# Gated delta-rule layer on one core: key products of two chunks side by side in one bank, and the triangular inverse built up from the identity

## The chip, the cores and the metric

The kernel runs on one core of one Trainium2 chip. The metric is the time on the device in microseconds (us) for one execution, as the median over several runs. Before the change it is 2536.91 us (three runs, 2536.58 to 2537.79).

## What is computed

The input x has 4 sequences of 512 tokens with 256 features. After a layer norm it goes through a gated delta rule with 16 query/key heads, each shared by 2 value heads of 128 features, and through a small gated feed-forward part whose weights come from a table of 16 numbers; the result is x plus the product of both. The part that matters here, for every pair of sequence and value head, works on chunks of 64 tokens:

```python
q, k = rmsnorm(q) * inv, rmsnorm(k) * inv              # and q, k, v from a conv and silu
decay = where(tril, exp(g[..., :, None] - g[..., None, :]), 0.0)
M = where(stril, einsum('bhncd,bhnmd->bhncm', k_beta, k) * decay, 0.0)
T = solve_triangular(eye + M, eye, lower=True)          # 64 x 64 for each chunk
v_c, k_cumdecay = T @ v_beta, T @ (k_beta * exp(g))
# then a scan over the 8 chunks: attn = (q_i @ k_i^T) * dec_i, v_new = v_i - kcd_i @ state, ...
```

## The kernel before, in words

The work is cut into 32 rounds. A round takes one query/key head and two of the four sequences (BB = 2), and so 8 chunks (NC = 8) of each of two sequences for two value heads (RATIO = 2). The two value heads lie in the two halves of the 128 partitions, 64 rows (C = 64) each. In a round each engine goes through the same three parts, in an order written out by hand, and the engines meet by semaphores: `invert`, `recur`, and `begin` of the following round.

- `begin` makes what the inverse needs. TensorE multiplies keys by keys and queries: tile `kq` holds for each chunk the keys twice and the queries once (3 x 64 columns). L481 takes the 128 columns with the doubled keys as weights and the 128 columns of keys and queries as moving data. So the product stands in both partition halves, one copy for each value head, 4 chunks in a PSUM bank, 4 banks in all (uses "kkq"). VectorE multiplies the key part of each bank by -DB (decay and beta) into U (L1009) and by -DB0 (the same, only for pairs of neighbouring tokens) into X (L1010). ScalarE copies the query part into A (L792). GpSimd has made DB0 from DB earlier, in `first_level` (L1180). After its 4 banks VectorE scales the last output block of the round before (`scale_o(last, 3)`, L1093, tile `on`), adds the identity to X (L1018), does `gated(last, 3)` (L1104) and turns X into W within the blocks (L1033).
- TensorE goes on in `begin` with the turned keys (L487, uses "kt", copied out by ScalarE at L783 into Kd), then `turn_back(last, 3)` (L641), which waits for `scale_o(last, 3)`, then the turned values (L494, uses "vt", copied out by ScalarE at L800 into V with a factor for each row). Then follow three of the four output products of the round before (L651).
- `invert` doubles the inverted blocks in 5 levels: two groups of 64 by 64 products in each (L462 and L464, then L467 and L469), with a ScalarE copy of the first result (L814), a masked copy of the second into X by VectorE (L1045), a turn (L1033), and `swap`, a ScalarE copy of X with the halves exchanged (L836). Beside the levels TensorE makes the projections of the next round (L413), ScalarE and VectorE their convolution (`tap0` L732, `taps` L948).
- `recur` is the scan over the chunks (L591, L599, L617, L564, L569 on TensorE; L1064, L1083, L961 and others on VectorE; squares for the output norm on ScalarE, L855; Sd at L1188 and small powers at L1204, L1214 on GpSimd).

A PSUM bank is handed over by counters: `wait_open` waits until the last reader is through with it, `wait_full` until TensorE has filled it. Which use lies in which bank is set in `bank_uses`. The weights `w_o`, `w_qkv` and the small rows come by DMA from SyncE's queue; the constants (identity, masks) are one transfer at the start, which ScalarE, TensorE and GpSimd wait for. TensorE also increments a semaphore `tiled` ahead of each group of 64 by 64 products; nothing waits for it.

Of the kernel before, what the change touches and what calls it, by code (L numbers as in the profile page):

```python
# [9 lines left out]
I32 = mybir.dt.int32  # L10
# [68 lines left out]
def constants():  # L79
# [3 lines left out]
    cols.append(((j // 2 == i // 2) & (j % 2 == 0) & (i % 2 == 1)) * 1.0)  # L83
    for lv in range(1, LEVELS):
# [9 lines left out]
NCONST = 2 * P + C + C + (LEVELS - 1) * HALF + C + 4  # L94
# [35 lines left out]
def build(nc, x, consts, resets_in, wqkvz, wba, convw, dtb, alog, normw, wout, lut, idx, out):  # L130
# [3 lines left out]
    with ExitStack() as ctx:  # L134
# [22 lines left out]
        DB0 = sb("DB0", [P, BB, NC, C])  # L157
# [32 lines left out]
        def flat(t, n=None):  # L190
# [7 lines left out]
        first_mask = cst[:, 2 * P + C:2 * P + 2 * C]  # L198
        masks = [cst[:, 2 * P + 2 * C + HALF * n:2 * P + 2 * C + HALF * (n + 1)] for n in range(LEVELS - 1)]
# [13 lines left out]
                 "normed_o dec_pool dec_small ss_c dec_act qg_c sd_c kg_c a_c u_c xs eye_c st_c x_c o_sq ff_gu ff_gate ff_h ff_y ff_sy fin x_again stored tiled").split()  # L213
# [42 lines left out]
        gw = [t for buf in (DB, DB0, Dm) for t in (flat(buf, S)[:, 0, :], flat(buf, S)[:, 1, :])]  # L256
# [9 lines left out]
        def _(sp):  # L266
# [56 lines left out]
            def body(R):  # L323
# [10 lines left out]
                if R.par == 1 and not R.nxt:  # L334
                    wait_read(sp, R, "kkq", 3)
# [33 lines left out]
        def _(pe):  # L369
# [75 lines left out]
            def products(banks, lv, first):  # L445

                pe.sem_inc(s["tiled"], 1)
# [96 lines left out]
            def keys_through(R):  # L544

                for b in range(BB):
# [3 lines left out]
                    pe.sem_inc(s["tiled"], 1)  # L550
# [23 lines left out]
            def recur(R):  # L574
# [3 lines left out]
                for b in range(BB):  # L578
                    bank, filled = wait_open(pe, R, "vn", b)
                    pe.sem_inc(s["tiled"], 1)  # L580
# [4 lines left out]
                for c in range(NC):  # L585
# [22 lines left out]
                    if c < NC - 1:  # L608
                        _, s_filled = wait_open(pe, R, "sp", c)
                        for b in range(BB):  # L610
                            wait_read(pe, R, "vn", c * BB + b)
                            pe.sem_inc(s["tiled"], 1)
# [7 lines left out]
                    else:  # L620
                        for b in range(BB):
                            wait_read(pe, R, "vn", c * BB + b)
                        pe.sem_inc(s["tiled"], 1)
# [81 lines left out]
        def _(act):  # L705
            act.wait_ge(s["ld_const"], 16 * n_const)
            for t in range(NT):
                act.wait_ge(s["ln_stat"], 2 * (t + 1))
                act.activation(std[:, t:t + 1], mv[:, t, 1:2], ACT.Sqrt, bias=eps[:, 0:1]).then_inc(s["ln_std"], 1)
# [43 lines left out]
            def decays(R):  # L753
                par = 0 if R.head else 1 - R.par
                act.wait_ge(s["dec_pool"], R.at(1, 9, 9))
# [6 lines left out]
                for b in range(BB):  # L762
                    act.wait_ge(s["dec_pool"], R.at(3 + 2 * b, 9, 9))
# [22 lines left out]
            def begin(R):  # L786
                for i in range(4):
                    act.wait_ge(s["u_c"], R.at(i + 1, 0, 4))
                    n, _ = R.use("kkq", i)
                    b, c4 = i // 2, slice((i % 2) * 4, (i % 2) * 4 + 4)  # L790
                    src = ps[n][:, :].rearrange("p (c t) -> p c t", t=P)
                    act.activation(A[:, b, c4, :], src[:, :, C:P], ACT.Copy).then_inc(read[n], 1)  # L792
# [3 lines left out]
                for i in range(4):  # L796
                    bank, done = wait_full(act, R, "vt", i)
                    for u in range(4):
                        c = (i % 2) * 4 + u
                        m = act.activation(V[:, i // 2, c, :], bank[:, u * P:(u + 1) * P], ACT.Copy,  # L800
                                           scale=rinv[:, i // 2, c:c + 1])
                    m.then_inc(done, 1)
                swap(R, 0)

            def invert(R):
                for lv in range(1, LEVELS):
# [31 lines left out]
            def body(R):  # L838
# [36 lines left out]
        def _(dve):  # L875
# [124 lines left out]
            def begin(R, last=None):  # L1000

                dve.wait_ge(s["dec_pool"], R.at(0, 9, 9))
# [31 lines left out]

            def invert(R):
                if R.before() is not None:
                    outputs(R.before(), (3,))
                for lv in range(1, LEVELS):
                    done = [wait_full(dve, R, "p2", (lv, b))[1] for b in range(BB)]
                    n = 1 << lv  # L1040

                    odd = X[:, :, :, :].rearrange("p b c (q d n) -> p b (c q) d n", d=2, n=n)[:, :, :, 1, :]

                    dve.memset(carry[:, 1:2], 0.0)
# [289 lines left out]
```

## Time and profile before

| | |
|---|---|
| median of 3 runs | 2536.91 us |
| the profiled execution, its own time | 2537.4 us |
| its span, first to last instruction | 2535.6 us |
| mean granted TensorE clock | 0.99 of full |
| busy: TensorE, weight loads, VectorE, ScalarE, GpSimd | 95%, 73%, 66%, 56%, 71% |
| one round in the middle of the run | 71.9 us |

The profile comes from one execution. "PE" is TensorE's products, "PEld" its weight loads, which overlap them, "DVE" is VectorE, "ACT" ScalarE, "POOL" GpSimd. A row of instructions gives how many there were, how long one took, and in square brackets how long the engine had been idle before it and what ended that. The chain of waits is followed back from the last instruction: at each step to what released it. In float32 most products are two instructions in the records, so 16 products are "x32".

### The profile page before, as it was taken

The page shows a single profiled execution, that of the slowest core. Times are in us where ns is not written, and L with a number is a line of the kernel's source. Part 1 is how long each engine was busy: PE and PEld are TensorE (multiplying, and loading weights), DVE is VectorE, ACT ScalarE, POOL GpSimd, SP SyncE. Part 2 cuts the span into 40 slices and gives each one's busy share as a digit, 9 for nine tenths or more (in the row PEclk, how much of TensorE's full clock was granted, in tenths as well). Part 3 has the DMA queues.
Part 4 walks back from the last instruction along what each step waited for, and adds up shares of the span by engine and source line. Part 5 has one row for each costly group of instructions (what it writes and reads, how often), then busy time and mean ns, then how long its engine had stood idle before and what let it go on. Part 6 is the DMA issues. An engine that isn't in the chain of part 4 may idle for free.

```text
span 2535.6 us, 102175 instructions
## 1 busy us (share of the span) xinstructions
PE 2403.8 (95%) x44496; PEld 1858.4 (73%) x44496; DVE 1663.7 (66%) x2955; ACT 1424.9 (56%) x3237; POOL 1809.7 (71%) x1838
## 2 busy tenths in 40 slices
PE   4899999999999999999999999999999999999899
PEld 3687777777877777777777777777777777776544
DVE  6666676667666766677666766676667666775322
ACT  2665565665656656656556566555566566564211
POOL 2787777778877777788777777787777777887200
PEclk8899999999999999999999999999999999999999
DMA  3111110111111101111111101111111011111100
GB/s 114 34 36 37 38 34 18 34 43 30 37 37 38 38 13 39 34 43 30 36 39 34 31 21 43 34 34 36 38 39 34 18 34 43 30 37 26 49 17 17
DMA packets 71051, 89.94 MB, mean 35 GB/s; under 512 B 16720, under 2 KB 39376, under 8 KB 70480
## 3 DMA queue, kind: packets, MB, share of 16 engines
q1 hardware_dynamic: 70608, 83.40, 12.4%
q8 instruction: 355, 5.82, 0.9%
q14 instruction: 88, 0.72, 0.1%
HBM read 78.30 MB, written 5.08 MB: 33 GB/s over the span
## 4 chain that ended last, share of the span: by engine, by line
PE 66%; DVE 23%; issue 5%; ACT 4%; DMA 1%; POOL 0%; DVEq 0%; SPq 0%; ACTq 0%; POOLq 0%
PE ps_two L433 9%; PE ps_two L651 9%; PE ps_two L413 9%; DVE cacc L948 7%; PE ps_p L591 5%; DVE XW L1033 3%; PE ps_state L617 3%; PE ps_two L641 3%; PE ps_p L467 3%; PE ps_two L425 3%; ACT cacc L732 3%; DVE hT L1104 3%; PE ps_p L481 2%; DVE Vn L1064 2%; PE ps_p L599 2%
## 5 line engine op out<-in xcount | busy, mean ns | idle before, releaser
L1188 POOL TENSOR_TENSOR Sd<-St,el 128x512 f32<-128x512 f32 x192 | 201.3, 1048 | 455.9 <-ACT eg L758 358.4
L1226 POOL TENSOR_SCALAR hT<-idx_s,lutb 128x134 f32<-128x134 int32 x480 | 355.5, 744 | 27.1
L1064 DVE TENSOR_SCALAR Vn<-ps_p,bR 128x128 f32<-128x128 f32 x512 | 165.3, 348 | 266.9 <-PE ps_p L564 180.0
L836 ACT ACTIVATE Xs<-XW 64x512 f32<-64x512 f32 x320 | 201.1, 628 | 233.2 <-DVE XW L1045 227.6
L948 DVE SCALAR_TENSOR_TENSOR cacc<-ps_two,cw,cacc 128x1022 f32<-128x1022 f32 (+2 forms) x192 | 243.1, 1266 | 73.0 <-ACT cacc L732 69.9
L948 DVE SCALAR_TENSOR_TENSOR cacc<-ps_state,cw,cacc 128x1022 f32<-128x1022 f32 (+2 forms) x192 | 244.3, 1273 | 31.1 <-ACT cacc L732 13.5
L413 PE MATMUL ps_state<-xnT,w_qkv 128*128 128x256 f32 x1024 | 257.1, 395 | 5.9 <-DVEq L953 5.9
L433 PE MATMUL ps_two<-xnT,w_z 128*128 128x512 f32 x512 | 244.4, 610 | 8.9 <-DVEq L953 8.2
L413 PE MATMUL ps_two<-xnT,w_qkv 128*128 128x256 f32 x1024 | 247.0, 389 | 0.0
L651 PE MATMUL ps_two<-w_o,hT 128*128 128x256 f32 x1024 | 236.3, 384 | 0.0
L1033 DVE STREAM_TRANSPOSE XW<-XW 128x1024 f32<-128x1024 f32 x160 | 199.3, 1245 | 36.5 <-DVE XW L1045 31.5
L462 PEld LDWEIGHTS ps_p<-XW,U 64*64 64x64 f32 (+1 forms) x5120 | 156.5, 130 | 76.6 <-issue 76.2
L413 PEld LDWEIGHTS ps_state<-xnT,w_qkv 128*128 128x128 f32 x1024 | 185.9, 191 | 34.6 <-DVEq L953 6.3
L651 PEld LDWEIGHTS ps_two<-w_o,hT 128*128 128x128 f32 x1024 | 190.6, 191 | 25.0
L855 ACT ACTIVATE P<-ps_p 128x128 f32<-128x128 f32 x256 | 67.2, 277 | 249.8 <-PE ps_p L569 249.8
L413 PEld LDWEIGHTS ps_two<-xnT,w_qkv 128*128 128x128 f32 x1024 | 187.4, 190 | 27.5
L467 PEld LDWEIGHTS ps_p<-XW,P 64*64 64x64 f32 (+1 forms) x5120 | 151.8, 129 | 71.0 <-issue 71.0
L591 PE MATMUL ps_p<-St,Kg 128*64 128x128 f32 x1792 | 161.3, 292 | 34.1 <-DVE St L1083 30.6
L462 PE MATMUL ps_p<-XW,U 64*64 64x32 f32 (+1 forms) x5120 | 173.6, 215 | 18.0 <-DVE XW L1033 13.3
L1199 POOL TENSOR_TENSOR qg<-qg,kq 128x512 f32<-128x512 f32 x128 | 190.7, 1522 | 0.0
L1083 DVE TENSOR_TENSOR St<-Sd,ps_state 128x256 f32<-128x256 f32 x384 | 144.4, 417 | 49.6 <-PE ps_state L617 19.1
L1113 DVE TENSOR_TENSOR acc<-acc,ps_two 128x512 f32<-128x512 f32 x128 | 86.8, 678 | 135.5 <-PE ps_two L651 135.5
(166 smaller groups left out, 6237.5 us busy)
## 6 DMA issues: line engine op xcount, KB each, us to landing
qg<-g_scratch SPq DMA_DIRECT2D x64, 512.0 KB, 7.3
g_st<-g_scratch SPq DMA_DIRECT2D x64, 256.0 KB, 5.6
w_qkv<-in_wqkvz SPq DMA_DIRECT2D x16, 512.0 KB, 3.8
w_z<-in_wqkvz SPq DMA_DIRECT2D x16, 256.0 KB, 3.1
w_o<-in_wout SPq DMA_DIRECT2D x16, 256.0 KB, 2.7
idx_s<-in_idx SPq DMA_DIRECT2D x32, 67.0 KB, 1.8
fw_scratch<-looked_up SPq DMA_DIRECT2D x32, 67.0 KB, 1.7
Kg<-in_x SPq DMA_DIRECT2D x2, 1024.0 KB, 6.0
```

What stands on the lines that cost most here:

```text
L413: m = pe.matmul(bank[:, t0:t0 + S // 2], w_qkv[:, k, kind * P:(kind + 1) * P], rows, start=(k == 0), stop=(k == KD - 1))
L433: m = pe.matmul(bank[:, :], w_z[:, k, a * P:(a + 1) * P], xnT[:, k, cols(R.par, b)], start=(k == 0), stop=(k == KD - 1))
L462: left = pe.matmul(to(0, m_same), U[k_same, 0, c, ins], halves(W[k_same, 0, c, :], lv, 0), start=True, stop=True)
L467: left = pe.matmul(to(0, k_same), P1[m_same, 0, c, k0:k0 + kn], halves(X[m_same, 0, c, :], lv, 1), start=True, stop=True)
L591: m = pe.matmul(olds[b][0][r, 0:P], Kg[:, b, c, r], St[:, cur, b, a, :], start=False, stop=True, skip_group_check=True)
L651: m = pe.matmul(bank[:, b * D:(b + 1) * D], hT[:, t, b, 1 - a, :], w_o[:, a, :], start=(a == 0), stop=(a == RATIO - 1))
L836: act.activation(Xs[(1 - a) * C:(2 - a) * C], X[a * C:(a + 1) * C, 1], ACT.Copy).then_inc(s["x_c"], 1)
L948: dve.scalar_tensor_tensor(dst, both[n][:, :, 0:S - t], cw[:, kind, 3 - t:4 - t], dst, ALU.mult, ALU.add).then_inc(s["taps"], 1)
L1033: dve.transpose(flat(W), flat(X)).then_inc(xs, 1)
L1064: dve.tensor_scalar(Vn[:, cur, b], bank[:, 0:P], bR[:, R.par, b, c:c + 1], None, ALU.mult).then_inc(done, 1)
L1188: pool.tensor_tensor(Sd[:, :, :, :], St[:, c % 2, :, :, :], el[:, R.par, :, :, c].unsqueeze(3).broadcast_to([P, BB, RATIO, P]), ALU.mult). ...
L1226: m = pool.tensor_scalar(slots[k], idx_s[:, :], float(k), lutb[:, k:k + 1], ALU.is_equal, ALU.mult)
```

## The change

Key products: each chunk's product now has only 64 weight columns, and two chunks stand side by side in the partition halves of one bank, so that 2 banks hold what 4 held. VectorE and ScalarE read each half and write it to both halves of U and A. The first level of the inverse no longer goes through DB0: ScalarE writes the identity into all blocks of X (once at the start, and near the end of each `recur`), and VectorE lays the odd rows of U over it with a masked copy. The mask of that level becomes as long as those of the others, 512 columns for 64. DB0 and its GpSimd work go. ScalarE copies half of the turned values in `begin`, the other half inside level 1. The increments of `tiled` go, here and at five more places in `keys_through` and `recur`. The banks of "kt" and "vt" are dealt out anew.

```diff
-    begin = (spread([("kkq", i) for i in range(4)], (4, 5, 6, 7)) + spread([("kt", i) for i in range(4)], (2, 4, 5, 6))
-             + spread([("vt", i) for i in range(4)], (3, 7, 2, 4)))
+    begin = (spread([("kkq", b) for b in range(BB)], (4, 5)) + spread([("kt", i) for i in range(4)], (2, 6, 7, 4))
+             + spread([("vt", i) for i in range(4)], (3, 5, 7, 6)))
...
-NCONST = 2 * P + C + C + (LEVELS - 1) * HALF + C + 4
+NCONST = 2 * P + C + LEVELS * HALF + C + 4
...
@@ TensorE, products @@
-                pe.sem_inc(s["tiled"], 1)
...
@@ TensorE, begin @@
-                for i in range(4):
-                    bank, filled = wait_open(pe, R, "kkq", i)
+                for b in range(BB):
+                    bank, filled = wait_open(pe, R, "kkq", b)
                     for u in range(4):
-                        c = (i % 2) * 4 + u
-                        m = pe.matmul(bank[:, u * P:(u + 1) * P], kq[:, i // 2, c, 0:P], kq[:, i // 2, c, C:3 * C],
-                                      start=True, stop=True)
+                        for side in range(2):
+                            c = side * 4 + u
+                            m = pe.matmul(bank[side * C:(side + 1) * C, u * P:(u + 1) * P], kq[:, b, c, 0:C],
+                                          kq[:, b, c, C:3 * C], start=True, stop=True)
                     m.then_inc(filled, 1)
...
@@ ScalarE @@
+            def clear_inverse():
+                act.activation(X[:, :].rearrange("p b c i -> p (b c) i"), eye.unsqueeze(1).broadcast_to([P, BB * NC, C]),
+                               ACT.Copy).then_inc(s["eye_c"], 1)
+
+            clear_inverse()
...
             def begin(R):
-                for i in range(4):
-                    act.wait_ge(s["u_c"], R.at(i + 1, 0, 4))
-                    n, _ = R.use("kkq", i)
-                    b, c4 = i // 2, slice((i % 2) * 4, (i % 2) * 4 + 4)
-                    src = ps[n][:, :].rearrange("p (c t) -> p c t", t=P)
-                    act.activation(A[:, b, c4, :], src[:, :, C:P], ACT.Copy).then_inc(read[n], 1)
+                for b in range(BB):
+                    bank, _ = wait_full(act, R, "kkq", b)
+                    for side in range(2):
+                        act.wait_ge(s["u_c"], R.at(2 * b + side + 1, 0, 4))
+                        src = bank[side * C:(side + 1) * C, :].rearrange("p (c t) -> p c t", t=P)[:, :, C:P]
+                        for a in range(RATIO):
+                            m = act.activation(A[a * C:(a + 1) * C, b, side * 4:side * 4 + 4, :], src, ACT.Copy)
+                    m.then_inc(read[R.use("kkq", b)[0]], 1)
                 for i in range(4):
                     copy_turned(R, "kt", i, Kd)
                 act.wait_ge(s["rinv_c"], R.at(0, 1, 1))
-                for i in range(4):
+                values(R, 0)
+                swap(R, 0)
...
@@ ScalarE, invert: after the copy of level 1 @@
+                    if lv == 1:
+                        values(R, 1)
...
@@ ScalarE, recur part of body @@
+                    if c == NC - 1 and R.nxt:
+                        for b in range(BB):
+                            wait_full(act, R, "vn", (NC - 1) * BB + b)
+                        clear_inverse()
...
@@ VectorE, begin @@
-                for i in range(4):
-                    if i == 2 and last is not None:
+                for b in range(BB):
+                    if b == 1 and last is not None:
                         gated(last, 2)
-                    bank, _ = wait_full(dve, R, "kkq", i)
-                    b, c4 = i // 2, slice((i % 2) * 4, (i % 2) * 4 + 4)
-                    src = bank[:, :].rearrange("p (c t) -> p c t", t=P)[:, :, 0:C]
-                    dve.scalar_tensor_tensor(U[:, b, c4], src, -1.0, DB[:, b, c4, :], ALU.mult, ALU.mult)
-                    dve.scalar_tensor_tensor(X[:, b, c4], src, -1.0, DB0[:, b, c4, :], ALU.mult, ALU.mult
-                                             ).then_inc(s["u_c"], 1)
+                    bank, _ = wait_full(dve, R, "kkq", b)
+                    for side in range(2):
+                        c4 = slice(side * 4, side * 4 + 4)
+                        src = bank[side * C:(side + 1) * C, :].rearrange("p (c t) -> p c t", t=P)[:, :, 0:C]
+                        for a in range(RATIO):
+                            r = slice(a * C, (a + 1) * C)
+                            m = dve.scalar_tensor_tensor(U[r, b, c4], src, -1.0, DB[r, b, c4, :], ALU.mult, ALU.mult)
+                        m.then_inc(s["u_c"], 1)
                 if last is not None:
                     scale_o(last, 3)
                 for b in range(BB):
                     dve.wait_ge(s["u_c"], R.at(2 * b + 2, 0, 4))
-                over_all = eye.unsqueeze(1).broadcast_to([P, BB * NC, C])
-                x_all = X[:, :].rearrange("p b c i -> p (b c) i")
-                dve.tensor_tensor(x_all, x_all, over_all, ALU.add).then_inc(xs, 1)
+                dve.wait_ge(s["eye_c"], R.at(1, 0, 1))
+                into_odd(0, odd(U, 0)).then_inc(xs, 1)
...
+            def into_odd(lv, src):
+
+                dve.memset(carry[:, 1:2], 0.0)
+                mask = masks[lv].rearrange("p (b q n) -> p b q n", b=BB, n=1 << lv)
+                return dve.copy_predicated(odd(X, lv), mask.bitcast(I32), src)
...
@@ GpSimd @@
-            def first_level(R, b):
-                pool.wait_ge(s["dec_pool"], R.at(5 + b + 1, 9, 9))
-                pool.tensor_tensor(DB0[:, b, :, :], DB[:, b, :, :], first_mask.unsqueeze(1).broadcast_to([P, NC, C]),
-                                   ALU.mult).then_inc(s["dec_pool"], 1)
```

## Rows read from the trace of the kernel before

**Rows 1.** The page: shares of the chain of waits by engine.

```profile
PE 66%; DVE 23%; issue 5%; ACT 4%; DMA 1%; POOL 0%; DVEq 0%; SPq 0%; ACTq 0%; POOLq 0%
```

**Rows 2.** Chain of waits in one round: start us, us, what ended last there.

```profile
1018.50 1.80 PE ps_p L481 x16
...
1023.96 0.66 PE ps_two L641 x4
...
1026.36 5.18 PE ps_two L651 x24
...
1039.42 1.12 ACT cacc L732
```

**Rows 3.** Timeline of TensorE's weight loads there: start us, us, in brackets the idle time.

```profile
1023.12 0.47 PEld L487 LDWEIGHTS ps_state<-cst,kq 128*128 128x128 f32 x4
1023.95 0.42 PEld L641 LDWEIGHTS ps_two<-cst,on 128*128 128x128 f32 x4 [0.37 <-DVE on L1093]
...
1025.21 0.91 PEld L494 LDWEIGHTS ps_p<-cst,vs 128*128 128x128 f32 x8
```

**Rows 4.** The same chain at changes between product shapes.

```profile
1008.41 0.39 PE ps_p L591 x4
...
1016.76 0.44 PE ps_p L599 x8
...
1017.26 0.65 PE ps_p L569 x8
1017.92 0.59 PE ps_two L641 x4
...
1035.60 3.67 PE ps_two L413 x16
```

**Rows 5.** Timeline of VectorE through `begin`.

```profile
1019.52 0.42 DVE L1009 SCALAR_TENSOR_TENSOR U<-ps_p,DB 128x256 f32<-128x256 f32 x1 [0.86 <-PE ps_p L481]
...
1021.00 0.74 DVE L1104 SCALAR_TENSOR_TENSOR hT<-ps_two,gpar,z 128x512 f32<-128x512 f32 x1
1021.89 0.42 DVE L1009 SCALAR_TENSOR_TENSOR U<-ps_state,DB 128x256 f32<-128x256 f32 x1
...
1022.89 0.41 DVE L1010 SCALAR_TENSOR_TENSOR XW<-ps_state,DB 128x256 f32<-128x256 f32 x1
1023.22 0.68 DVE L1093 TENSOR_TENSOR on<-ps_p,rr 128x512 f32<-128x512 f32 x1
```

**Rows 6.** VectorE at L961, four in a row, each on other partition halves: together, and each.

```profile
1001.80 0.74 DVE L961 TENSOR_SCALAR kn<-ps_two 64x8 f32<-64x8 f32 x4
...
L961 DVE TENSOR_SCALAR kn<-ps_two x4: 146/164/170, 1001.8 to 1002.4; 64x8 f32<-64x8 f32 x4
```

**Rows 7.** Timeline of ScalarE through `begin` and level 1.

```profile
1017.95 0.28 ACT L855 ACTIVATE P<-ps_p 128x128 f32<-128x128 f32 x1 [3.73 <-PE ps_p L569]
...
1023.34 0.38 ACT L792 ACTIVATE A<-ps_state 128x256 f32<-128x256 f32 x1 [0.28 <-DVE XW L1010]
1023.62 1.57 ACT L783 ACTIVATE Kd<-ps_p 128x512 f32<-128x512 f32 x3
1025.05 0.63 ACT L783 ACTIVATE Kd<-ps_state 128x512 f32<-128x512 f32 x1
...
1027.52 2.27 ACT L800 ACTIVATE V<-ps_p,rinv 128x128 f32<-128x128 f32 x8
1029.81 1.28 ACT L836 ACTIVATE Xs<-XW 64x512 f32<-64x512 f32 x2
```

**Rows 8.** VectorE's and GpSimd's work that goes: by line, count, ns or total us.

```profile
L1018 DVE TENSOR_TENSOR XW<-XW,cst x32: 2039/2260/2314, 85.2 to 2319.0; 128x1024 f32<-128x1024 f32 x32
...
L1180 POOL TENSOR_TENSOR DB<-DB,cst 128x512 f32<-128x512 f32 x64 | 81.6, 1275 | 0.0
```

**Rows 9.** The start: the constants' transfer, and pieces of the chain of waits.

```profile
cst<-in_consts SPq DMA_DIRECT2D x1, 1506.0 KB, 11.0
...
87.50 4.11 ACT V L800 x16
```

More of the change, by code:

```diff
@@ L82, in constants @@
     cols = [np.eye(P), np.ones((P, P)), (j == i) * 1.0]
-    cols.append(((j // 2 == i // 2) & (j % 2 == 0) & (i % 2 == 1)) * 1.0)
-    for lv in range(1, LEVELS):
+    for lv in range(LEVELS):
         n = 1 << lv
@@ L197, in build @@
         eye = cst[:, 2 * P:2 * P + C]
-        first_mask = cst[:, 2 * P + C:2 * P + 2 * C]
-        masks = [cst[:, 2 * P + 2 * C + HALF * n:2 * P + 2 * C + HALF * (n + 1)] for n in range(LEVELS - 1)]
+        masks = [cst[:, 2 * P + C + HALF * n:2 * P + C + HALF * (n + 1)] for n in range(LEVELS)]
         causal = cst[:, NCONST - 4 - C:NCONST - 4]
@@ L212, in build @@
                  "ba_act g_c g_dup g_tr g_sc g_out fw_c fw_st ld_fw ld_fd zeroed tap0 taps silu sq n2_c rinv_c inv_o turned scaled "
-                 "normed_o dec_pool dec_small ss_c dec_act qg_c sd_c kg_c a_c u_c xs eye_c st_c x_c o_sq ff_gu ff_gate ff_h ff_y ff_sy fin x_again stored tiled").split()
+                 "normed_o dec_pool dec_small ss_c dec_act qg_c sd_c kg_c a_c u_c xs eye_c st_c x_c o_sq ff_gu ff_gate ff_h ff_y ff_sy fin x_again stored").split()
         s = {n: sem(n) for n in names}
@@ L255, in build @@
         scs = flat(z)[:, 0:1024].rearrange("p (k h b c) -> p k h b c", k=2, h=HQK, b=B)
-        gw = [t for buf in (DB, DB0, Dm) for t in (flat(buf, S)[:, 0, :], flat(buf, S)[:, 1, :])]
+        gw = [t for buf in (DB, U, Dm) for t in (flat(buf, S)[:, 0, :], flat(buf, S)[:, 1, :])]
         resets = flat(P1, S)[:, 1, :]
@@ L334, in body @@
                 if R.par == 1 and not R.nxt:
-                    wait_read(sp, R, "kkq", 3)
+                    wait_read(sp, R, "kkq", 1)
                     wait_read(sp, R, "kt", 3)
@@ L549, in keys_through @@
                     banks = [wait_open(pe, R, "kcd", 2 * b + a) for a in range(RATIO)]
-                    pe.sem_inc(s["tiled"], 1)
                     for c in range(NC):
@@ L579, in recur @@
                     bank, filled = wait_open(pe, R, "vn", b)
-                    pe.sem_inc(s["tiled"], 1)
                     for a in range(RATIO):
@@ L611, in recur @@
                             wait_read(pe, R, "vn", c * BB + b)
-                            pe.sem_inc(s["tiled"], 1)
                             for a in range(RATIO):
@@ L622, in recur @@
                             wait_read(pe, R, "vn", c * BB + b)
-                        pe.sem_inc(s["tiled"], 1)
                     for b in range(BB):
@@ L795, in begin, with values @@
                 act.wait_ge(s["rinv_c"], R.at(0, 1, 1))
-                for i in range(4):
+                values(R, 0)
+                swap(R, 0)
+            def values(R, b):
+                for i in range(2 * b, 2 * b + 2):
                     bank, done = wait_full(act, R, "vt", i)
@@ L799, in begin @@
                         c = (i % 2) * 4 + u
-                        m = act.activation(V[:, i // 2, c, :], bank[:, u * P:(u + 1) * P], ACT.Copy,
-                                           scale=rinv[:, i // 2, c:c + 1])
+                        m = act.activation(V[:, b, c, :], bank[:, u * P:(u + 1) * P], ACT.Copy,
+                                           scale=rinv[:, b, c:c + 1])
                     m.then_inc(done, 1)
-                swap(R, 0)
             def invert(R):
@@ L1033, in turn, with odd @@
                 dve.transpose(flat(W), flat(X)).then_inc(xs, 1)
+            def odd(t, lv):
+                return t[:, :, :, :].rearrange("p b c (q d n) -> p b (c q) d n", d=2, n=1 << lv)[:, :, :, 1, :]
+            def into_odd(lv, src):
+                dve.memset(carry[:, 1:2], 0.0)
+                mask = masks[lv].rearrange("p (b q n) -> p b q n", b=BB, n=1 << lv)
+                return dve.copy_predicated(odd(X, lv), mask.bitcast(I32), src)
             def invert(R):
@@ L1170, in with_beta @@
                 if not R.head and b == 0:
-                    wait_full(pool, R, "kkq", 3)
+                    wait_full(pool, R, "kkq", 1)
                     pool.wait_ge(s["u_c"], R.at(4, 0, 4))
@@ L1253, in attention @@
                 for b in range(BB):
-                    wait_read(pool, R, "kkq", 2 * b + 1)
+                    wait_read(pool, R, "kkq", b)
                     pool.tensor_tensor(A[:, b], A[:, b], Dm[:, b], ALU.mult).then_inc(s["a_c"], 1)
@@ L1260, in _ @@
                 with_beta(HEAD, b)
-            for b in range(BB):
-                first_level(HEAD, b)
             lengths(HEAD)
@@ L1277, in body @@
                         with_beta(R, c - 3)
-                    elif R.nxt and c > 4:
-                        first_level(R, c - 5)
                 if R.nxt:
```

15 lines of the change are left out of this document (5 added, 10 removed).

## The prediction

> **What bounds the kernel now.** I read the chain of waits first. TensorE holds 66% of it, VectorE 23% [rows 1]. A faster TensorE stage therefore pays only where no other engine ends the wait behind it. So I cut out one round, around `begin`, where the change lies, and asked of each engine when it starts what.
>
> The chain of waits goes there through the first key bank, then leaves TensorE: VectorE's eight products, `gated(last, 2)` and `on` follow and end at 1023.90 [rows 5], and only then `turn_back` (L641) runs. From 1023.96 TensorE holds the chain without a gap through the turned values, the outputs and level 1, until ScalarE's `tap0` at 1039.42 [rows 2]. The reader should see the handover: TensorE was through with loading the turned keys at 1023.12 + 0.47 = 1023.59 and its loads sat idle 0.37 us for `on` [rows 3]. TensorE, 95% busy over the run, has slack exactly where its work is cut, and whatever delays `on` moves the round. There are 31 such handovers between 32 rounds, and the weight loads' idle time ahead of L641 recurs in other rounds.
>
> **Key products on TensorE.** Now 16 products in 32 records, 16 of them in 1.80 us, so all in 3.6 us [rows 2]. After, 16 products with 64 weight columns in 8 pairs. The nearest row is L599: 4 products of this shape (64 columns, 128 moving) in 0.44 us on the chain [rows 4], 0.22 a pair. So 8 pairs cost 1.76 and save 1.8 us of TensorE's time. They bring a change of shape. In rows 4 the first pair after one takes 0.39 for 0.22 (L591 behind L641), so 0.17 us. The first bank, with 4 pairs, is full after 0.17 + 0.88 = 1.05 us, where the old one with 4 products took 0.90: VectorE starts 0.15 later, at 1019.67. The 1.8 us come out behind this, ahead of a wait for `on`, and give nothing by themselves. The Trainium skill ("TensorEngine Tiling (Array Packing)", Key Properties) says that a change of tiling mode drains TensorE; the 0.17 us agree with that. Its section on the PSUM bottleneck says that such packing doesn't speed up evacuation, and that is the case here by the handover of rows 2.
>
> **VectorE's eight products.** Their number stays 8, two for each old bank before, four for each new bank after, 256 elements each as before. Half the partitions don't shorten one; I keep 0.42 us. What changes is how they follow one another. Now they overlap: a piece that starts at 1022.89 and takes 0.41 is followed at 1023.22, 0.33 later, by `on` [rows 5]. The new ones read and write changing partition halves. The only row with this very pattern (half by half from PSUM, written to both halves) is L961: four take 0.74 together, 0.164 each, so (0.74 - 0.164) / 3 = 0.192 from start to start, 0.03 more than the length [rows 6]. They don't overlap. ScalarE's L836 shows the same: two take 1.28, so 0.64 each or a little more, against (1025.05 - 1023.62) / 3 = 0.48 from start to start for L783's full-height copies of the same 512 elements [rows 7]. I take 0.42 + 0.03 = 0.45 for each of the eight; the other bound is 0.335, as now. Between them I choose by L961, whose pattern is the same.
> The Trainium skill ("VectorE: DVE Perf Modes", Two Vector instructions with no wait between them) says that an instruction whose start quadrant differs from the last one's, in what it reads or writes, starts only when all earlier ones have finished. By it every new product is held, which gives the sum below; L961's spacing agrees. If it failed here, the time would be that of rival 1.
>
> VectorE's clock: 1019.67 + 4 x 0.45 = 1021.47; `gated` 0.89 to the next start (1021.00 to 1021.89, rows 5) 1022.36; 4 x 0.45 gives 1024.16, where `on` started at 1023.22. So `on`, and L641 with it, comes 0.94 us later.
>
> **ScalarE and the banks.** The second turned-value group of TensorE's last four (L494 x8) needs "vt" 2 in bank 7, where "kt" 2 stands until ScalarE has copied it; before, it needed "kt" 0, copied long ago. ScalarE: last U piece starts at 1023.71, ends 1024.13; the copy into A starts 0.04 later as now (1022.89 + 0.41 to 1023.34), then again, each 0.38 + 0.02 without overlap; "kt" 0 starts at 1024.98, "kt" 2 two steps of 0.48 later at 1025.94, and ends 0.61 after that (1.57 for three less two steps), at 1026.55 [rows 7]. TensorE would be there at 1025.21 + 0.94 = 1026.15 [rows 3]. It waits until 1026.60 and then needs 0.66 + 0.44 = 1.10 us for the two groups (restart as L641, then as L599's 0.44) and ends at 1027.70, where it ended at 1026.36 before. **The handover costs 1.34 us a round.** Bounds of the ScalarE part alone: nothing if its copies keep pace, 0.4 as worked here. Behind it everything up to `tap0` is TensorE's own time, so nothing takes the delay back.
>
> **The rest.** (a) L1018, 2.26 us [rows 8], becomes a masked copy of 512 elements. It lies behind `on`; the turned X is wanted at 1031.5, VectorE has it by 1028.5 before and after, so nothing. If that cover of 3 us were gone it would gain 1 to 1.5 us. (b) GpSimd loses two L1180 a round, 2.55 us [rows 8]. It only comes to its powers and `scale_q` earlier; `on` isn't waiting for it. Nothing. (c) ScalarE's identity, 1024 elements, 1.1 us as `tap0`, as large [rows 2], waits for the last Kg product (done at 1016.76, where L599 begins, rows 4) and runs until 1017.9, in the 3.73 us of idleness ahead of L855 at 1017.95 [rows 7]. Nothing, at most 0.1 on the squares, whose result has 2 us of slack. (d) Eight of the 16 copies into V, half of 16 x 0.283 us (L800's 2.27 for 8, rows 7), move behind level 1's copy: ScalarE waits there for X until 1037. Hidden. (e) Removing `tiled`: into 64 by 64 shapes, with the increment, the first group costs 0.65 - 0.43 = 0.22 (L569); without it, into full shape, 0.59 - 0.43 = 0.16 (L641) and 3.67 - 3.41 = 0.26 (L413, 16 of 0.213) [rows 4]. No difference, so nothing; bounds 0 and 0.04 us for each of 29 in a round, of which about 20 lie on the path. (f) Start: 224 KB more constants on 1506 KB in 11.0 us [rows 9], +1.6 at most, the first identity +1.0, against 4.11 / 2 = 2.05 less ahead of the first level [rows 9] and some 1 us of products at the low clock. Together 0, within 3.
>
> **Sum.** 2537.4 (the profiled execution; span 2535.6) + 31 x 1.34 = 41.5 gives 2578.9. The runs' median lies 0.5 below that execution: 2578.4, so 2578 us.
>
> **Rivals.**
> 1. *VectorE's products keep overlapping.* Then `on` is late by 0.15 - 0.14 (the small wait for the second bank goes) = 0.01 only; "kt" 2 is copied by 1025.48 and TensorE loses 0.27 us: 31 x 0.27 = 8.4, 2545 us. For: the pieces share no data. Against: L961's and L836's spacing. Chance 0.12, with what lies between it and the forecast.
> 2. *Faster: the removed increments were not free.* They stand in TensorE's queue, and a standing cost of 0.04 us each, 20 on the path, 32 rounds, is 26 us; with rival 1's small loss the time is 2519. Its place is ahead of L462, L467, L617; it decides the sign once it exceeds what the handover costs. Against: rows 4 show no dearer entry with it. The other way to gain, that TensorE's saved 1.8 us show (31 x 1.8 = 56 us, 2481), needs `on` to be early, against 0.37 us of waiting for it [rows 3]. Chance of both 0.10.
> 3. *The pairs don't run side by side*, the edit does not do what it says. Then the first bank is full 0.88 us later again and the handover costs 2.2 us: 2606. Against: L599. Chance 0.04.
> 4. *About no change*, gains and losses cancelling: 0.04.
>
> The forecast has 0.70. A measurement of this kernel can tell about 0.2%, 5 us, from no change. The range goes down to rival 1 (2545) and up to 1.8 us a round, 0.5 us a piece in place of 0.45 and the late start in full, 2593. Faster 0.10, same 0.05 (rival 4 and a part of rival 1), slower 0.85.
>
> **What would show it.** L1009's new pieces: 8 a round, 0.42 long, 0.45 apart, where overlap would show 0.34. TensorE's loads idle about 3 us ahead of L641, ended by `on`, and again about 0.4 ahead of L494, ended by ScalarE's Kd. L481 in 8 pairs at 0.22. Rounds of 73.2 us for 71.9. Wrong I would be if the pieces were shorter than 0.42, or if the rounds were shorter while `on` is late: then a cost that I put at nothing, `tiled` first, was one.

## The result and the profile after

The changed kernel takes 2604.35 us (median of 4, 2602.49 to 2605.87) against 2536.76 for the kernel before; the ratio is 1.0265, 95% interval [1.0247, 1.0283]. It is slower by 67.6 us, where 41 us were forecast. The direction and the place were right, the size was not: the time lies above the range, which ended at 2593.

The page after, its span, granted clock in 40 slices and chain of waits, against [rows 1]:

```profile
span 2604.1 us, 101789 instructions
...
PEclk8999999999999999999999999999999999999999
...
PE 62%; DVE 25%; issue 5%; ACT 4%; DVEq 0%; DMA 0%; ACTq 0%; POOL 0%; POOLq 0%; SPq 0%
```

The slices are too coarse for what counts. The mean granted clock is 0.977, where it was 0.990.

Here is one handover between rounds, in the timeline of the weight loads (start us, us, idle time in brackets). It answers to [rows 3], with 102.00 us between corresponding moments of the two traces (the loads of the turn before the key products start at 1017.85 and at 1119.85):

```profile
1119.85 0.42 PEld L634 LDWEIGHTS ps_two<-cst,on 128*128 128x128 f32 x4 [0.17 <-DVE on L1109]
1120.44 1.73 PEld L478 LDWEIGHTS ps_p<-kq 128*64 128x64 f32 x32 [0.17 <-issue]
...
1124.27 0.42 PEld L484 LDWEIGHTS ps_p<-cst,kq 128*128 128x128 f32 x4 [0.64 <-ACT A L792]
1126.86 0.42 PEld L634 LDWEIGHTS ps_two<-cst,on 128*128 128x128 f32 x4 [2.18 <-DVE on L1109]
...
1128.54 0.86 PEld L491 LDWEIGHTS ps_state<-cst,vs 128*128 128x128 f32 x8 [0.39 <-ACT Kd L782]
1129.37 0.73 PEld L644 LDWEIGHTS ps_two<-w_o,hT 128*128 128x128 f32 x4
```

The wait for `on` grew from 0.37 to 2.18 us, and there are two new ones, 0.64 for the bank that ScalarE's A copies free and 0.39 for "kt" 2. VectorE's timeline over the same stretch, as in [rows 5]:

```profile
1121.67 1.75 DVE L1023 SCALAR_TENSOR_TENSOR U<-ps_p,DB 64x256 f32<-64x256 f32 x4 [1.04 <-PE ps_p L478]
1123.45 0.75 DVE L1120 SCALAR_TENSOR_TENSOR hT<-ps_two,gpar,z 128x512 f32<-128x512 f32 x1
1124.34 1.74 DVE L1023 SCALAR_TENSOR_TENSOR U<-ps_p,DB 64x256 f32<-64x256 f32 x4
1126.12 0.69 DVE L1109 TENSOR_TENSOR on<-ps_p,rr 128x512 f32<-128x512 f32 x1
```

and ScalarE's, as in [rows 7]:

```profile
1118.83 1.06 ACT L702 ACTIVATE XW<-cst 128x1024 f32<-128x1024 f32 x1 [2.65 <-PE ps_p L586]
1119.96 0.28 ACT L866 ACTIVATE P<-ps_p 128x128 f32<-128x128 f32 x1
...
1125.28 1.61 ACT L792 ACTIVATE A<-ps_p 64x256 f32<-64x256 f32 x4 [1.07 <-DVE U L1023]
```

Four pieces take 1.75 us, so (1.75 - 0.42) / 3 = 0.44 from start to start. The identity (L702) fits exactly before the squares. In this handover the forecast is met to a tenth: pieces from 1121.67 - 102.00 = 1019.67 (forecast 1019.67), L634's loads from 1024.86 (1024.89), the second pair of turned values from 1026.54 (1026.60). The interval from this round's first piece back to the one before is long, 75.03 us, the next one is 73.20, the length that I had forecast for all.

The next handover looks like this:

```profile
1197.47 0.42 PEld L484 LDWEIGHTS ps_p<-cst,kq 128*128 128x128 f32 x4 [0.64 <-ACT A L792]
1200.07 0.54 PEld L634 LDWEIGHTS ps_two<-cst,on 128*128 128x128 f32 x4 [2.18 <-DVE on L1109]
1200.60 1.72 PEld L491 LDWEIGHTS ps_p<-cst,vs 128*128 128x128 f32 x8
1202.30 1.60 PEld L491 LDWEIGHTS ps_state<-cst,vs 128*128 128x128 f32 x8
```

The waits are the same, but the turned values' loads take 1.72 us, where before the change they took 0.91 [rows 3]. The stretches of the two handovers, with each engine's busy time and, ahead of the DMA share, the granted clock:

```profile
1125.00:1129.00 4.00, 1.98 (x16) 1.75 (x17) 3.64 (x7) 3.60 (x9) 3.25 (x3) 1.00 0.80 192
...
1199.00:1203.00 4.00, 2.93 (x15) 2.93 (x16) 3.54 (x6) 3.89 (x11) 3.25 (x3) 0.66 0.83 163
1203.00:1207.00 4.00, 4.00 (x21) 3.64 (x20) 1.37 (x2) 3.92 (x9) 4.00 (x3) 0.91 0.53 150
```

In the second TensorE is at its lower level, 1.2 GHz instead of 2.4, for (1 - 0.66) x 4 / 0.5 + (1 - 0.91) x 4 / 0.5 = 3.4 us. What it did before was to idle 2.2 us. After this wait TensorE works without a pause until level 1, some 9 us, so half of the 3.4 us, 1.7, is lost. The 0.39 us for "kt" 2 fall away in return, as in the rows above, and the round gets longer by 1.3. Of the 30 intervals between first pieces from 152.94 to 2382.99 us, 7 are 73.2 to 73.3 us, all without low clock, and 23 are 74.4 to 75.2, each with one stretch of 3.4 us. The wait for `on` is 2.2 us in every handover but one (2.5), so the same wait does not always bring the clock down. The low clock is the term that the forecast did not have.

### The profile page after: what moved, and what is told of

It is laid out like the page before. It is cut to its first block, busy times and chain, and to the rows that moved or that the text cites. A ratio compares the mean times of both kernels' runs of the same rounds, so it can differ in the third digit from the quotient of the medians.

```text
span 2604.1 us, 101789 instructions
## 1 busy us (share of the span) xinstructions
PE 2392.6 (92%) x44496; PEld 1826.4 (70%) x44496; DVE 1658.2 (64%) x2987; ACT 1514.8 (58%) x3398; POOL 1707.2 (66%) x1774
## 4 chain that ended last, share of the span: by engine, by line
PE 62%; DVE 25%; issue 5%; ACT 4%; DVEq 0%; DMA 0%; ACTq 0%; POOL 0%; POOLq 0%; SPq 0%
PE ps_two L430 9%; PE ps_two L644 9%; PE ps_two L410 8%; DVE cacc L959 8%; PE ps_p L586 5%; DVE U L1023 4%; DVE XW L1045 3%; PE ps_state L611 3%; PE ps_two L634 3%; PE ps_p L463 3%; ACT cacc L731 3%; DVE hT L1120 3%; PE ps_two L422 3%; DVE Vn L1080 2%; PE ps_p L594 2%
## 5 line engine op out<-in xcount | busy, mean ns | idle before, releaser
L644 PE MATMUL ps_two<-w_o,hT 128*128 128x256 f32 x1024 | 243.3, 392 | 0.0
L644 PEld LDWEIGHTS ps_two<-w_o,hT 128*128 128x128 f32 x1024 | 197.8, 199 | 26.6
L410 PEld LDWEIGHTS ps_state<-xnT,w_qkv 128*128 128x128 f32 x1024 | 186.3, 192 | 37.3 <-DVEq L964 12.0
L458 PEld LDWEIGHTS ps_p<-XW,U 64*64 64x64 f32 (+1 forms) x5120 | 150.5, 129 | 66.4 <-DVE XW L1045 45.5
L458 PE MATMUL ps_p<-XW,U 64*64 64x32 f32 (+1 forms) x5120 | 168.2, 215 | 9.6 <-DVE XW L1045 5.7
L463 PE MATMUL ps_p<-XW,P 64*64 64x32 f32 (+1 forms) x5120 | 168.7, 215 | 1.9 <-ACTq L822 1.9
L465 PE MATMUL ps_p<-Xs,P 64*64 64x32 f32 (+1 forms) x5120 | 169.1, 216 | 0.0
```

The source lines that it names most:

```text
L410: m = pe.matmul(bank[:, t0:t0 + S // 2], w_qkv[:, k, kind * P:(kind + 1) * P], rows, start=(k == 0), stop=(k == KD - 1))
L458: left = pe.matmul(to(0, m_same), U[k_same, 0, c, ins], halves(W[k_same, 0, c, :], lv, 0), start=True, stop=True)
L463: left = pe.matmul(to(0, k_same), P1[m_same, 0, c, k0:k0 + kn], halves(X[m_same, 0, c, :], lv, 1), start=True, stop=True)
L644: m = pe.matmul(bank[:, b * D:(b + 1) * D], hT[:, t, b, 1 - a, :], w_o[:, a, :], start=(a == 0), stop=(a == RATIO - 1))
```

## The experiments

Each kernel is the changed one with one edit, if not said otherwise; each time is a median of at least 4 runs. The kernel before took 2536.6 to 2537.7 us beside them.

**The increments of `tiled` put back** (29 in a round).

```diff
             def products(banks, lv, first):
+                pe.sem_inc(s["tiled"], 1)
...
                     bank, filled = wait_open(pe, R, "vn", b)
+                    pe.sem_inc(s["tiled"], 1)
```

> The changed kernel with the 29 increments of `tiled` a round put back. My theory (they cost nothing; the loss is the late `on` plus stretches of low clock behind TensorE's idle time): 2604 us, within 4. Rival (the increments held TensorE's order or its shape changes in a good way, so their removal is part of the loss): 2585 us or less. Rival (they cost something and their removal gave a hidden gain): 2620 to 2630 us.

2607.88 us, ratio 1.0277 [1.0260, 1.0294], which overlaps the changed kernel's. The increments are worth nothing that can be measured, in either direction.

**TensorE's idle time filled with products.**

```diff
-                    for u in range(4):
+                    for u in range(4 * (6 if i == 3 and last is not None else 1)):
+                        u = u % 4
                         m = pe.transpose(bank[:, u * P:(u + 1) * P], kq[:, i // 2, (i % 2) * 4 + u, 0:P], ident)
```

> The changed kernel, but TensorE turns the last group of keys six times instead of once, into the same bank, so that about 2.1 of the 2.3 us of idle time ahead of `turn_back(last, 3)` are filled with products; nothing that another engine does is changed, and the result is the same. My theory (the low clock, some 23 stretches of 3.4 us at half, follows on the idle time): the stretches go, `on` is as late as before, rounds of 73.2 us, so 2604 - 23 x 1.3 = 2574 us. Rival (the narrow paired products themselves, or something else in the stage, lower the clock): the stretches stay, 2604 us or more, as the added products lie in idle time. If the filling delays L634 itself: up to 0.3 us a round more than that.

2574.69 us, ratio 1.0143 [1.0128, 1.0159], mean granted clock 0.993. The same moment in the timeline of the weight loads:

```profile
1109.94 1.67 PEld L485 LDWEIGHTS ps_p<-cst,kq 128*128 128x128 f32 x15
1111.60 0.44 PEld L635 LDWEIGHTS ps_two<-cst,on 128*128 128x128 f32 x4
```

and the stretch behind it, with the granted clock (1.00) ahead of the DMA share:

```profile
1112.00:1116.00 4.00, 3.87 (x28) 3.43 (x27) 3.11 (x3) 3.98 (x13) 3.28 (x3) 1.00 0.99 241
```

Work that nobody needs makes the kernel 29.7 us faster. VectorE's and ScalarE's work is unchanged, so `on` comes as late as before; only the idle time is gone, and with it the low clock between rounds. This divides the loss: 2574.7 - 2536.8 = 37.9 us at full clock, for which 41 were forecast, and 29.7 us for the clock.

**The banks of the last two turned-value groups exchanged** ("vt" in banks 3, 5, 6, 7 for 3, 5, 7, 6).

> The changed kernel with the banks of the last two turned-value groups exchanged, so that the third waits for `kt` 1 and not `kt` 2 to be copied. My theory (this wait costs 0.38 us a round by the trace of the changed kernel): TensorE's second wait goes, 31 x 0.38 = 12 us less, 2592 us, and down to 2575 if fewer stretches of low clock follow. Rival (the wait is covered, the round is set by `on` alone): 2604 us.

2598.26 us, 6 less. The wait is gone (L491's second group starts at 1124.84, right behind the first), but it gave half of the 12 us:

```profile
1123.58 0.42 PEld L634 LDWEIGHTS ps_two<-cst,on 128*128 128x128 f32 x4 [2.17 <-DVE on L1109]
1123.96 0.91 PEld L491 LDWEIGHTS ps_p<-cst,vs 128*128 128x128 f32 x8
1124.84 0.91 PEld L491 LDWEIGHTS ps_state<-cst,vs 128*128 128x128 f32 x8
```

The trace of the changed kernel shows why. Where the low clock starts early, its first group takes 1.72 us, and by then "kt" 2 is copied, as the rows at 1200.60 and 1202.30 show. The wait for it stands in only 14 of the 31 handovers (in 7 of the 23 with a low stretch), and 14 x 0.39 = 5.5 us. Without this wait to cover, a low stretch costs its full 1.7 us: the rounds here take 72.8 us at full clock (a few 73.2) and 74.5 or more with the stretch. The mean clock stayed at 0.978.

**`scale_o(last, 3)` ahead on VectorE, nothing else.**

```diff
                     if b == 1 and last is not None:
+                        scale_o(last, 3)
                         gated(last, 2)
...
-                if last is not None:
-                    scale_o(last, 3)
```

> The changed kernel with `scale_o(last, 3)` moved ahead on VectorE and nothing else. Theory A (two things are late, `on` and ScalarE's copies that free the banks of the turned values): `turn_back` runs 2 us earlier, but the turned values wait for ScalarE, whose last copies into A now start 0.3 us later; TensorE idles as long, in another place: 2595 to 2615 us. Rival B (`on` is the only cause): 2535 to 2560 us.

2629.57 us, above both ranges. `on` is no longer waited for, and the idle time has moved behind it, larger than I had worked out:

```profile
1056.88 0.42 PEld L634 LDWEIGHTS ps_two<-cst,on 128*128 128x128 f32 x4 [0.53 <-issue]
1057.27 0.47 PEld L491 LDWEIGHTS ps_p<-cst,vs 128*128 128x128 f32 x4
1059.45 0.42 PEld L491 LDWEIGHTS ps_p<-cst,vs 128*128 128x128 f32 x4 [1.72 <-ACT A L792]
1061.05 1.55 PEld L491 LDWEIGHTS ps_state<-cst,vs 128*128 128x128 f32 x8 [1.18 <-ACT Kd L782]
```

`on` in front of the second group of pieces pushes that group back by its whole 0.84 us, and ScalarE's A copies and "kt" copies with it; I had put 0.3. Here 31 x 0.8 = 25 us, the measured difference; the low clock costs as much as before (18 stretches of 1.7 us in 30 rounds for 23 of 1.3). So `on` alone is not the cause. The chain is VectorE's pieces, ScalarE's copies, banks.

**`gated(last, 2)` moved into VectorE's 1.04 us of idle time ahead of the first key bank.**

```diff
                 dve.wait_ge(s["dec_pool"], R.at(0, 7, 7))
+                if last is not None:
+                    gated(last, 2)
                 for b in range(BB):
-                    if b == 1 and last is not None:
-                        gated(last, 2)
```

> The changed kernel with one move: VectorE does `gated(last, 2)` while it waits for the first key bank (1.04 us idle there) instead of between its two groups of pieces. `on`, and ScalarE's copies behind the second group, come 0.9 us earlier. My theory (VectorE's chain up to `on` sets the round, and the length of TensorE's idle time the low clock): 31 x 0.9 = 28 us less by the chain, 2576 us, and if the shorter idle time of 1.4 us no longer brings the clock down, 30 more, 2546 us. Rival (ScalarE or the banks set the round): less than 10 us saved.

2546.86 us, ratio 1.0041 [1.0028, 1.0054]: 57.5 us less from one moved call, as worked out with both terms. The timeline of the weight loads in one handover:

```profile
1094.48 0.42 PEld L484 LDWEIGHTS ps_p<-cst,kq 128*128 128x128 f32 x4 [0.72 <-ACT A L792]
1096.18 0.42 PEld L634 LDWEIGHTS ps_two<-cst,on 128*128 128x128 f32 x4 [1.28 <-DVE on L1109]
```

and the stretch around it, with the granted clock (1.00) ahead of the DMA share:

```profile
1094.00:1098.00 4.00, 2.32 (x17) 1.85 (x18) 3.63 (x7) 3.70 (x10) 4.00 (x4) 1.00 0.90 164
```

With 1.28 us idle for 2.18 the clock stays whole (mean 0.994), and no low stretch lies between the first and the last handover. The rounds take 72.4 us for 73.2, so 31 x 0.8 = 25 us come from the chain and the clock's 30 us on top.

**The change's inverse without its key products**: full-height banks and VectorE's four full-height pieces, the rest as changed, except that all V copies stay in `begin` (with these banks the split would make TensorE and ScalarE wait for each other).

```diff
-                    for side in range(2):
-                        c4 = slice(side * 4, side * 4 + 4)
-                        src = bank[side * C:(side + 1) * C, :].rearrange("p (c t) -> p c t", t=P)[:, :, 0:C]
-                        for a in range(RATIO):
-                            r = slice(a * C, (a + 1) * C)
-                            m = dve.scalar_tensor_tensor(U[r, b, c4], src, -1.0, DB[r, b, c4, :], ALU.mult, ALU.mult)
-                        m.then_inc(s["u_c"], 1)
+                    b, c4 = i // 2, slice((i % 2) * 4, (i % 2) * 4 + 4)
+                    src = bank[:, :].rearrange("p (c t) -> p c t", t=P)[:, :, 0:C]
+                    dve.scalar_tensor_tensor(U[:, b, c4], src, -1.0, DB[:, b, c4, :], ALU.mult, ALU.mult
+                                             ).then_inc(s["u_c"], 1)
```

> The kernel before with its four full-height key banks, and of the change only the inverse from the identity (no DB0, ScalarE's identity, masked copy; all V copies stay in `begin`; no increments). VectorE has 4 full-height pieces in place of 8, so `on` comes 4 x 0.33 = 1.3 us earlier than before and TensorE no longer waits for it. My theory (the half-height pieces are what made the change slower): no slower than before; the 0.37 us of waiting goes, some 0.2 to 0.4 us a round, 2525 to 2532 us, clock as before. Rival (the identity, its wait or the first masked copy cost something): above 2540 us.

2525.34 us, ratio 0.9949 [0.9935, 0.9964]: faster than both kernels. The wait for `on` is gone:

```profile
1019.03 0.47 PEld L483 LDWEIGHTS ps_state<-cst,kq 128*128 128x128 f32 x4
1019.47 0.47 PEld L633 LDWEIGHTS ps_two<-cst,on 128*128 128x128 f32 x4
```

The inverse from the identity is worth 11 us by itself; VectorE has half as many pieces ahead of `on`, the wait for it goes, and rounds take 71.6 us for 71.9. The key products, with their banks and the split of the V copies, gave this away and 68 us more.

**Half-height pieces in two orders**, on that kernel. Each full-height piece is cut into its partition halves (source and target in the same half), once alternating, once with the half kept for two or more in a row. The diff shows the orders of (bank, half) in the two groups.

```diff
+(((0, 0), (0, 1), (1, 0), (1, 1)), ((0, 0), (0, 1), (1, 0), (1, 1)))
...
+(((0, 0), (1, 0), (1, 1), (0, 1)), ((0, 1), (1, 1), (1, 0), (0, 0)))
```

> The full-height key banks and identity inverse (2525 us), but each of VectorE's four full-height pieces is cut into its two partition halves, in the order low, high, low, high. Nothing else halves; ScalarE and TensorE have full height. My theory (a piece that changes partition half does not overlap with the one before): 8 pieces 0.44 us apart, four take 1.75, as in the changed kernel; `on` about 2 us later than with four pieces and TensorE waits for it: 2555 to 2575 us. Rival (what kept the pieces apart in the changed kernel is something else, the mixed source and target halves or the bank shared by two chunks): pieces 0.33 apart, at most 2540 us.

> The same eight half-height pieces of the same lengths, in an order that keeps the half for two or more in a row (low, low, high, high, then high, high, low, low). My theory (only the change of half is held): inside a half 0.33 us apart, at the change 0.44; four take 1.55 for 1.75, so `on` comes 0.3 to 0.4 us earlier than in the alternating order, 8 to 15 us less than it. Rival (half-height pieces are never overlapped): the same time as the alternating order, within 3 us.

2601.76 and 2584.20 us. First the pieces, a group of four in each order (alternating, then grouped):

```profile
1046.72 1.75 DVE L1019 SCALAR_TENSOR_TENSOR U<-ps_p,DB 64x256 f32<-64x256 f32 x4 [1.75 <-PE ps_p L477]
```

```profile
1039.53 1.53 DVE L1019 SCALAR_TENSOR_TENSOR U<-ps_p,DB 64x256 f32<-64x256 f32 x4 [1.75 <-PE ps_p L477]
```

1.75 and 1.53 us were worked out as 1.75 and 1.55. Inside a half the pieces overlap as full-height ones do (0.34 or 0.35 us from start to start), at a change they do not (0.42 to 0.45), and this holds with source and target in one half and one chunk in a bank. So the size of a piece is not the reason, the change of half is. The Trainium skill ("VectorE: DVE Perf Modes", Two Vector instructions with no wait between them) says that an instruction with another start quadrant than the last one's waits until the earlier ones have finished; these two runs agree. The grouped order is 17.6 us faster, a little more than forecast: 31 x 0.44 = 14 us by the two groups (rounds of 73.4 us for 73.8), and the alternating order had two stretches of low clock, 1.9 us each, that the grouped one does not have.

The absolute time of the alternating order was forecast 27 to 47 us too low. I had made ScalarE wait for a whole group and VectorE for both its banks, and had overlooked that the last "kt" group needs bank 6, that is, the third A copy:

```profile
1051.69 0.42 PEld L483 LDWEIGHTS ps_state<-cst,kq 128*128 128x128 f32 x4 [1.89 <-ACT A L790]
```

These two kernels say how pieces follow each other, not what the changed kernel's time would be.

**`begin` reordered.** `scale_o(last, 3)` ahead as above, three "kt" copies ahead of the second half of A on ScalarE, "vt" 1 to 3 in banks 2, 6 and 7, which these copies free.

```diff
-             + spread([("vt", i) for i in range(4)], (3, 5, 7, 6)))
+             + spread([("vt", i) for i in range(4)], (3, 2, 6, 7)))
...
-                for i in range(4):
-                    copy_turned(R, "kt", i, Kd)
+                    for i in (range(3) if b == 0 else (3,)):
+                        copy_turned(R, "kt", i, Kd)
```

> The changed kernel with the order of `begin` mended: VectorE does `scale_o(last, 3)` behind its first four pieces, ScalarE copies three groups of turned keys before the second half of A, and turned values 1 to 3 go to banks 2, 6 and 7, which those copies free. The half-height pieces stay. My theory (the pairs save TensorE 1.8 us, and they only cost because `on` and the copies came late): TensorE goes through `begin` with gaps under 0.5 us, the clock stays full, about 1.0 us a round less than before: 2500 to 2512 us. Rival (the half-height pieces cost the round wherever they stand, for example by the turn of X for level 1): 2550 us or more.

2534.30 us (10 runs), ratio 0.9991 [0.9982, 1.0001], 70 us less than the changed kernel, but not the 2500 to 2512 forecast. Rounds take 71.8 us, so the half-height pieces do not cost the round wherever they stand. Of the gaps in `begin`, 0.64 us ahead of the last "kt" group and about 0.5 ahead of `turn_back` are left, the 2.18 are gone, and a new wait stands in the outputs:

```profile
1025.14 1.59 PEld L644 LDWEIGHTS ps_two<-w_o,hT 128*128 128x128 f32 x8 [0.58 <-DVE hT L1119]
```

**Two more moves**: `gated(last, 2)` as above, and `gated(last, 3)` ahead of the masked copy.

```diff
+                if last is not None:
+                    gated(last, 3)
                 into_odd(0, odd(U, 0)).then_inc(xs, 1)
-                if last is not None:
-                    gated(last, 3)
```

> The reordered kernel of e5 with two more moves on VectorE: `gated(last, 2)` ahead of the first key bank as in e10, and `gated(last, 3)` ahead of the masked copy, because in e5 the second output product waited 0.58 us for it. My theory (what e5 lacked of the 1.0 us a round is this wait): TensorE from `turn_back` to level 1 without a wait but 0.4 us ahead of the last turned keys, 1.3 us a round less than the kernel before: 2496 us, 2490 to 2510. Rival (level 1 then waits for X or its turned copy): about e5's 2534 us, not below 2520.

2510.30 us (2509.34 to 2511.54), ratio 0.9893 [0.9878, 0.9907], the fastest of all, just outside the expectation's 2490 to 2510 and 14 us above its value of 2496. A round takes 70.9 us for 71.9, where I had expected 70.6. What is missing: the last "kt" group waits 0.72 us for ScalarE, not 0.64, and in 4 of 32 rounds the masked copy takes 2.92 to 2.95 us instead of 1.43 to 1.46, with output products waiting behind it; these rounds take 72.7 us, and 4 x 1.7 = 7 of the 14 us are theirs. (The last "kt" group waits 1.07 us in these four.) VectorE, GpSimd and TensorE in such a round, in their timelines:

```profile
1014.63 2.95 DVE L1055 COPY_PREDICATED XW<-cst,U 128x512 f32<-128x512 int32 x1 [0.18 <-DVE hT L1120]
```

```profile
1014.51 1.91 POOL L1260 TENSOR_TENSOR Kg<-Kd,eg 128x1024 f32<-128x1024 f32 x1
1016.36 2.78 POOL L1260 TENSOR_TENSOR Kd<-Kd,ed 128x1024 f32<-128x1024 f32 x1
```

```profile
1019.58 1.97 PE L644 MATMUL ps_two<-w_o,hT 128*128 128x256 f32 x8 [1.45 <-DVE acc L1129]
```

and VectorE and GpSimd in the next round, an ordinary one:

```profile
1087.32 1.44 DVE L1055 COPY_PREDICATED XW<-cst,U 128x512 f32<-128x512 int32 x1
```

```profile
1087.54 2.78 POOL L1260 TENSOR_TENSOR Kg<-Kd,eg 128x1024 f32<-128x1024 f32 x1
```

The fastest kernel is 15 us ahead of the full-height one (2525.34), so the key products can pay, once the order around them is right; the moves of `gated` were not tried on the full-height kernel.

## Why the prediction was wrong in size, step by step

- **Pairs on TensorE**: right. The pieces start at the forecast moment. The 1.8 us saved show only as idle time.
- **VectorE's pieces not overlapping, 0.45 apart**: right, 0.44 measured, and shown to hang on the change of half by the two orders.
- **Handover cost 1.34 us a round**: right as far as it went. Loads of L634 0.03 us earlier than forecast, the round 73.20 for 73.2; 37.9 us in all at full clock (the filled-gap kernel) for 41.5. The forecast took 71.9 us for every round before, but the first eight that it counts take 72.1 to 72.9, and the filled-gap kernel does not lengthen them by the full 1.34: the 30 intervals between first pieces come to 37.3 us more, 1.24 each. Why the early rounds are longer was not looked into.
- **ScalarE and the banks**: the 0.4 us for "kt" 2 is right. The wait of the last "kt" group for the A copies (0.64) was not in the text; it costs nothing where it is, ahead of a longer wait.
- **The failed step** is the sentence that everything behind the handover is "TensorE's own time", priced at full clock: the sum has no term for a lower clock behind the handovers, and no reason is given for that. I had even written that the loads would idle some 3 us. In 23 of 30 rounds the clock then goes to its lower level for 3.4 us, which costs 1.3 us each, 29.7 us by the filled-gap kernel. The profile before had the material for a bound: its granted clock falls only at the start and near the end, where TensorE idles 2.7 to 3.5 us at a time, and in no round between, where its loads idle 0.37 us for `on`. One of these places, TensorE's timeline and the two stretches with the granted clock ahead of the DMA share:

```profile
2390.43 0.65 PE L641 MATMUL ps_two<-cst,on 128*128 128x128 f32 x4 [2.73 <-DVE on L1093]
```

```profile
2388.00:2392.00 4.00, 1.57 (x7) 1.38 (x8) 1.93 (x3) 0.29 (x3) 1.21 (x2) 0.88 0.00 0
2392.00:2396.00 4.00, 4.00 (x14) 3.27 (x13) 0.69 (x1) 0.00 (x0) 0.00 (x0) 0.69 0.00 0
```

  That is again (0.12 + 0.31) x 4 / 0.5 = 3.4 us of the lower level. A range with such a stretch after every handover would have reached 2578 + 31 x 1.7 = 2631 and held the result. The Trainium skill ("TensorE: Matmul & The Clock Gate", Why this matters for your kernels) warns of idle gaps between bursts of products for this reason; I had not weighed it. The gaps it speaks of are longer than the 2.2 us, with another 0.6 shortly before, that were enough here in most rounds.
- **Nothing for `tiled`, GpSimd's 2.55 us, the identity, the V copies**: `tiled` shown by its run. The others hold by the trace after and, together, by the full-height kernel, which has all of them but the V split and is faster than before. GpSimd's work costs nothing by being less, but where it lies beside the masked copy counts, as said at the end.
- **Rivals**: rival 1 (pieces overlap) is refuted, rival 2's increments too, and rival 3 (pairs one after another) by L478's products: its loads take 1.73 us in all, for 8 pairs, as forecast. The time of rival 3, 2606, is near the measured one, by another cause: a right number would not have been a right reason.

## What to carry to other kernels

Before shortening work on an engine, see whose wait ends behind it: the 1.8 us went into idle time, and cutting VectorE's pieces into halves lengthened just the chain that TensorE waits for. A longer wait of TensorE can cost more than its length, since the products behind it may run at half clock; price it both ways. Pieces that change partition half one by one cost VectorE its overlap, so keep the half for as long as the order allows, and look first for work that fits into an idle stretch, which here gave 57 us with one moved call. Such a move can also put a copy of VectorE beside other work of GpSimd and change its length, so look at both timelines after it.

## What the runs showed of the hardware that was not expected

- TensorE at full clock fell to the lower level for 3.4 us after a wait of 2.2 us in most, not all, handovers with the same wait. Waits of its loads of 1.9 us brought it down in 2 of 31 handovers (alternating order). With waits of 0.7 and 1.3 us (`gated` moved) and with the wait filled it never fell between the first and the last handover; the mean clock was 0.994 and 0.993.
- A masked copy of 512 columns takes 0.72 us in the median with its data in PSUM (rows below, of the fastest kernel). The first level's, with its data in SBUF, took very different times, and GpSimd's tensor operations beside it go with them. With none under way, the copy takes 1.33 us (all 31 handovers of the alternating order). In nine kernels one is under way as the copy starts, and the copy ends 1.16 to 1.20 us after that operation ends, in every such round: 1.47 us long in the changed kernel, 1.95 in the full-height one, 2.30 in the one with `gated(last, 2)` moved alone, 1.44 in the fastest, and 2.92 to 2.95 in four of its rounds. There L1260 had started 0.13 us ahead of the copy and took its usual 1.9 us; in the other rounds it starts 0.22 us behind the copy and takes 2.8 itself (rows above). So these two work one after the other, and 0.3 us in the order of their starts decide over 1.5 us of VectorE's time. The order was not varied on purpose; the runs only happen to differ in it. The shortening against L1018's 2.26 us that I had put at 1 to 1.5 us by the element count is thus 0.8 in the changed kernel:

```profile
L1055 DVE COPY_PREDICATED XW<-cst,ps_p x160: 693/724/1318, 96.8 to 2336.9; 128x512 f32<-128x512 int32 x160
L1055 DVE COPY_PREDICATED XW<-cst,U x32: 1426/1444/2950, 87.1 to 2298.0; 128x512 f32<-128x512 int32 x32
```
